# Last states of the first attention round gathered group by group, and the first table made ahead of the other setup work

## The chip, the cores and the metric

The kernel runs on one core of a Trainium2 chip. The metric is the device time of one execution in microseconds (us); of several runs the median is taken. The engines are PE (TensorE), DVE (VectorE), ACT (ScalarE), POOL (GpSimd) and SP (SyncE, which here only issues DMAs); ACT issues DMAs too, and POOL issues the indirect ones (gathers).

## The reference

A graph with 3125 nodes of 64 features and 103,125 edges sorted by destination goes through four blocks, each followed by a residual add and a layer norm: a normalised sum, two attention layers, a relational layer with 16 edge types and an edge convolution of three layers with a maximum. In short:

```python
edge_index = jnp.stack([src, dst])
x = _layernorm(x + _L0_gnn_ref(x, edge_index), axis=-1)      
x = _layernorm(x + _L1_gnn_ref(x, edge_index, edge_attr, ...))
x = _layernorm(x + _L2_gnn_ref(x, weight, norm, src, dst, rel_type), axis=-1)
x = _layernorm(x + _L3_gnn_ref(x, edge_index, W1, b1, W2, b2), axis=-1)

def _transformer_conv(...):          # one attention round
    ke = k[src] + e
    score = jnp.sum(q[dst] * ke, axis=-1) / jnp.sqrt(64)
    a = jnp.exp(score - jax.ops.segment_max(score, dst)[dst])
    alpha = a / jax.ops.segment_sum(a, dst)[dst]
    out = jax.ops.segment_sum(alpha[:, None] * (v[src] + e), dst)
    return out + x @ ws + bs
```

## The kernel before

Edges are padded to 808 tiles of 128 and taken in 202 chunks of 4 tiles (`TC`, `EC` = 512 edges). There are seven rounds, numbered from 0: sum, attention, attention, relation, and three maxima; in the maxima a step takes one chunk of either half, so that they have 101 steps. A round has two parts.

In its **chunk part** POOL gathers the source rows of a chunk from a table in HBM (`src_table`, four gathers of 128 rows each, L1086 or L1093), PE turns them so that features lie in partitions, DVE runs a scan along the edges (L1562) that starts anew where the destination changes, PE turns the scan's states back, ACT copies them to `hb`, and ACT's queue stores them to `states_sum` or `states_att` (L1236). A node's result is then the state of its last edge. In an attention round there is more: windows of `dst_table` are loaded by SP, one-hots on PE spread the queries to the edges, scores are formed and reduced per group of four chunks, and the weighted rows are scanned with a decay. Each engine has one instruction stream per round, written by `chunks` as a loop over a ring of 8 chunks (4 in the maxima), with stages that lag by up to 13 chunks; semaphores join the streams. In an attention round POOL may run 8 chunks ahead of the weighted rows (`q.weighted`).

In its **node part** the 25 blocks of 128 nodes are taken in 7 groups (`GROUPS`, six of four blocks and one of one). POOL gathers the last states of each block into `agg` by the indices `last_i` (L1114, 25 gathers). DVE, PE and ACT then form the next round's features in the order of `STEPS`, group after group, staggered, and SP stores them as the next `src_table` and `dst_table`. The next round's first gather waits for these.

POOL's wait ahead of these gathers differs by round:

```python
if g < G - 1 and q.r > 1:
    ends = [nc.values_load(group_ends[...]) for e, m in ((g, most), (G - 1 + g, least))]
    wait(pool, *[(q.st_stored[s], ends[0] if s < q.steps % U else ends[1]) for s in range(U)])
elif g == G - 1 or not g:
    wait(pool, *[(q.st_stored[s], each * ((q.steps - s + U - 1) // U)) for s in range(U)])
```

From round 2 on, group g waits only for the number of stored chunks that its own last edge needs (`group_ends`, made by DVE in the setup); in rounds 0 and 1, group 0 waits for all chunks of the round.

**Setup.** DVE counts per node how many tiles begin at or before it (L1453), POOL gathers the tile in which each node ends (L1077), and DVE counts within it (`count_within`, L1445 to L1448), three groups (`LATE`) behind. That gives `edges_le`, from it the degrees (with PE, and a square root on ACT) and `zn`, the features scaled by the inverse root degree, which SP stores as the first `src_table` (L943). Around it stand on DVE the tile-wise base `base` (which ACT needs for its first indices), the mask `joint`, the relation indices, `w1`, the flags `tile_same`, `last_i`, and later `tile_pens`. SP's queue is in order: loads, five stores of zero rows (`dst_table<-zrow`, L934), flags (L938, L940), the table (L943), the penalties `pens` (L945, L947), and then round 0, whose first loads are L962 and L965.

Of the kernel before, what the change touches and what calls it, by code (L numbers as in the profile page):

```python
# [26 lines left out]
P = 128  # L27
TC = 4
EC = TC * P
# [28 lines left out]
def gnn_kernel(nc, src, typ, wgt, dst_row, dst_prev, dst_tile, first, edge_t, x, W, out):  # L58
# [22 lines left out]
    with ctx:  # L81
# [15 lines left out]
        zrow = sb("zrow", [P, 3 * KA], bf16)  # L97
# [118 lines left out]
        zeros_stored = sem("zeros_stored")  # L216
        first_loaded = sem("first_loaded")
# [249 lines left out]
        PRE_EDGES = 2 + NB + 5 * G + 10  # L467
        PRE_DEG = PRE_EDGES + 4
        PRE_SCALED = PRE_DEG + 2

# [412 lines left out]
        def _(sp):  # L883
# [48 lines left out]
            for r in range(NR):  # L932
                if width[r]:
                    sp.dma_start(dsts[r][NP:NT, :], zrow[:, 0:3 * width[r]]).then_inc(zeros_stored, 16)  # L934

            sp.wait_ge(flags_made, 2)
# [5 lines left out]
            sp.wait_ge(dve_pre, PRE_SCALED)  # L942
            sp.dma_start(srcs[0].rearrange("(b p) f -> p b f", p=P), zn[:, :, :]).then_inc(rounds[0].src_stored[0], 16)  # L943
            sp.wait_ge(pens_made, 8)
            sp.dma_start(pens[0:whole * P, :].rearrange("(b p) f -> p b f", p=P), tile_pens[:, 0:whole, :])\  # L945
                .then_inc(pens_stored, 16)
            sp.dma_start(pens[whole * P:T, :], tile_pens[0:T - whole * P, whole, :]).then_inc(pens_stored, 16)  # L947

            for q in rounds:
# [88 lines left out]
                if k == SUM:  # L1038
                    chunks(sp, q.steps, (0, fetch_batch), (0, fetch_edges), (3, store_edges), (U + 2, store_onehots),
                           ring=2 * U)  # L1040
                elif k == REL:
# [10 lines left out]
        def _(pool):  # L1052
# [28 lines left out]
            for q in rounds:  # L1081
# [38 lines left out]
        def _(act):  # L1120
# [10 lines left out]
            nc.scalar.activation(deg[:, :], deg[:, :], ACT.Sqrt).then_inc(act_pre, 1)  # L1131

            for q in rounds:
# [117 lines left out]
                if k == ATT:  # L1251
                    chunks(act, q.steps, (B + 2, kept), (B + 2, weights), (B + LW, weigh), (B + LW, decays), (0, indices_att),
# [174 lines left out]
        def _(dve):  # L1427
# [23 lines left out]
            for g, (b0, nb) in enumerate(GROUPS):  # L1451
# [7 lines left out]
                if g >= LATE - 1:  # L1459
                    count_within(g - LATE + 1)  # L1460

            dve.wait_ge(pool_pre, PRE_POOL)
            dve.wait_ge(loaded, 16 * N_LOADS)
            pre(nc.vector.tensor_scalar(base[:, :], first_f[:, :], node_id[:, 0:1], None, ALU.add))
            pre(nc.vector.tensor_copy(before_f[:, :], before_half[:, :]))
            pre(nc.vector.tensor_tensor(before_f[:, :], before_f[:, :], first_f[:, TH:TH + 1], ALU.is_equal))
            pre(nc.vector.tensor_scalar(joint[:, :], node_id[:, :], first_f[:, TH:TH + 1], before_f[:, :],
                                        ALU.is_equal, ALU.mult))
            pre(nc.vector.tensor_scalar(joint[:, :], joint[:, :], BIG, -BIG, ALU.mult, ALU.add))
            pre(nc.vector.memset(edges_le[:, 0:1], 0.0))  # L1470
            pre(nc.vector.tensor_scalar(mask[:, :], src_i[:, :], float(R), None, ALU.mult))
            pre(nc.vector.tensor_tensor(mask[:, :], mask[:, :], rel_i[:, :], ALU.add))
            pre(nc.vector.tensor_copy(rel_i[:, :], mask[:, :]))
            pre(nc.vector.tensor_tensor(w1[:, :, 0:D], w1a[:, :, :], w1[:, :, D:2 * D], ALU.subtract))
# [7 lines left out]
            for g in range(G - LATE + 1, G):  # L1482
                count_within(g)
            assert made[0] == PRE_EDGES
            pre(nc.vector.tensor_scalar(last_f[:, :], edges_le[:, 1:NB + 1], -1.0, 0.0, ALU.add, ALU.max))
            pre(nc.vector.tensor_copy(last_i[:, :], last_f[:, :]))
            dve.wait_ge(pe_pre, 7)
            pre(nc.vector.tensor_tensor(deg[:, :], edges_le[:, 1:NB + 1], bank(2, 0)[:, 0:NB], ALU.subtract))
            pre(nc.vector.tensor_scalar(deg[:, :], deg[:, :], 1.0, None, ALU.max))
            assert made[0] == PRE_DEG  # L1490
            dve.wait_ge(act_pre, 7)
            pre(nc.vector.reciprocal(dinv[:, :], deg[:, :]))
            pre(nc.vector.tensor_tensor(zn[:, :, :], xn[:, :, :], dinv[:, :].unsqueeze(2).to_broadcast([P, NB, D]),
                                        ALU.mult))
            assert made[0] == PRE_SCALED

# [225 lines left out]
```

## Time and profile before

| | us |
|---|---|
| median of 3 runs | 9922.08 |
| the runs | 9895.71 to 9936.42 |
| profiled execution, span from first to last instruction | 9918.4 |

Of the profiled execution no other time is given than its span, so the two are taken as one and the same; it lies 3.7 us under the median of the runs. Its stages, by the first gather of each round: setup to 64 us, sum to 1345, first attention to 2986, second attention to 4722, relation to 5980, maxima to 7295, 8613 and the end.

A row of a timeline is one instruction, or several merged: its start, its duration, engine and line, result and operands, shapes, and in brackets how long the engine was idle before it and what ended that. "remote" and "another core or an unknown queue" mean that the trace names no releaser. SPq and ACTq rows are DMA issues, not the transfers.

### The profile page before, as it was taken

The numbers are of one execution on the slowest core, as the hardware profiler recorded it, in microseconds if no ns is written. First come the engines' busy times: TensorE is split into PE (matmuls) and PEld (weight loads), VectorE is DVE, ScalarE is ACT, GpSimd is POOL, SyncE is SP. The second block draws the span as 40 slices with busy tenths as digits, with TensorE's granted clock in tenths as the row PEclk, the third lists the DMA queues.
The fourth block names the chain that finished last, engine by engine and source line by source line (L and its number), as shares of the span: only waits on it lengthen the run. The fifth ranks groups of instructions, "written<-read, shape, count | busy, mean of one in ns | idle before, by whom it ended". The sixth has DMA issues, their size and how long they took to land.

```text
span 9918.4 us, 123616 instructions
## 1 busy us (share of the span) xinstructions
PE 3937.1 (40%) x24024; PEld 2674.1 (27%) x24024; DVE 2471.0 (25%) x4351; ACT 2035.1 (21%) x6406; POOL 5554.5 (56%) x5874
## 2 busy tenths in 40 slices
PE   2333334443343433336222224444444444444443
PEld 1222223333342333334111112222222222222222
DVE  4333333333332333332222221111111111111112
ACT  1111123333332333333101111111111111111111
POOL 6666644454434444442666665666656666556665
PEclk9999995555555555555555555666656666566666
DMA  4444434454444444443222223333333333333333
GB/s 121 126 126 126 125 91 108 109 110 107 108 92 97 109 106 107 107 107 99 54 50 50 51 48 82 91 90 90 89 79 90 90 90 90 80 89 90 91 91 80
DMA packets 2188624, 925.94 MB, mean 93 GB/s; under 512 B 1608302, under 2 KB 2071734, under 8 KB 2182134
## 3 DMA queue, kind: packets, MB, share of 16 engines
q1 hardware_dynamic: 1080022, 458.65, 19.0%
q10 hardware_dynamic: 921120, 272.38, 11.7%
q0 software_dynamic: 187392, 193.93, 9.6%
q8 instruction: 30, 0.49, 0.0%
q14 instruction: 60, 0.49, 0.0%
HBM read 657.48 MB, written 266.58 MB: 93 GB/s over the span
## 4 chain that ended last, share of the span: by engine, by line
issue 30%; PE 20%; another core or an unknown queue 9%; SPq 7%; DVE 2%; DVEq 1%; ACT 1%; DMA 0%; ACTq 0%; POOL 0%; POOLq 0%
PE ps L1323 7%; PE ps L1398 5%; PE ps L1319 3%; SPq L1002 3%; PE ps L1406 2%; PE ps L675 1%; PE ps L1309 1%; DVEq L374 1%; SPq L996 1%; SPq L1004 1%; SPq L998 1%; DVE edges_a L1580 1%; DVE st L1562 0%; SPq L370 0%
## 5 line engine op out<-in xcount | busy, mean ns | idle before, releaser
L1086 POOL DMA_INDIRECT edges_a<-src_table,idx x4040 | 3829.6, 948 | 2501.2 <-issue 1163.6
L1093 POOL DMA_INDIRECT edges_a<-src_table,idx x1616 | 1524.7, 944 | 1626.7 <-ACT weighted L1209 1063.1
L1323 PE MATMUL ps<-sel,win_sb 128*64 128x128 fp8e4 x7272 | 749.7, 262 | 1704.9 <-issue 1703.6
L1562 DVE TENSOR_TENSOR_SCAN st<-pen,st,ps 128x512 f32<-128x512 f32 x300 | 384.0, 1280 | 3279.9 <-remote 2939.6
L1406 PE MATMUL ps<-ident,st 64*128 64x64 f32 (+2 forms) x4444 | 849.1, 339 | 655.0 <-DVE st L1562 333.8
L1406 PEld LDWEIGHTS ps<-ident,st 64*128 64x128 f32 (+2 forms) x4444 | 705.6, 207 | 1063.1 <-issue 1039.8
L1323 PEld LDWEIGHTS ps<-sel,win_sb 128*64 128x64 bf16 x7272 | 396.2, 126 | 2056.6 <-issue 2009.9
L1562 DVE TENSOR_TENSOR_SCAN st<-edges_a,st,ps 64x512 f32<-64x512 fp8e4 x402 | 510.5, 1270 | 1665.6 <-remote 1292.0
L1309 PE MATMUL ps<-ident,edges_a 128*64 128x128 f32 x1616 | 421.4, 416 | 985.2 <-DVE edges_a L1580 643.5
L1335 PE MATMUL ps<-win_sb,sel 128*128 128x97 bf16 x4848 | 473.8, 271 | 849.1 <-issue 771.5
L1163 ACT ACTIVATE hb<-ps 128x256 f32<-128x256 f32 (+1 forms) x808 | 348.4, 431 | 2000.1 <-remote 1082.1
L1390 PE MATMUL ps<-ident,weighted 128*97 128x128 f32 x1616 | 452.8, 433 | 615.9 <-issue 279.9
L1595 DVE TENSOR_TENSOR prod<-ps,edges_a 128x388 f32<-128x388 f32 x404 | 225.4, 558 | 1795.3 <-remote 1459.7
L1335 PEld LDWEIGHTS ps<-win_sb,sel 128*128 128x128 fp8e4 x4848 | 396.1, 135 | 909.9 <-issue 826.0
L1319 PE MATMUL ps<-ident,edges_a 128*128 128x128 f32 x1212 | 439.2, 362 | 425.3 <-issue 354.7
L1227 ACT ACTIVATE edges_a<-ps,b 128x512 f32<-128x512 f32 x303 | 208.2, 687 | 1658.0 <-remote 1498.9
L1390 PEld LDWEIGHTS ps<-ident,weighted 128*97 128x97 f32 x1616 | 337.5, 274 | 659.9 <-issue 640.2
L1562 DVE TENSOR_TENSOR_SCAN st<-decay,st,ps 97x512 f32<-97x512 f32 x402 | 511.5, 1272 | 10.4 <-PE ps L1406 10.4
L1309 PEld LDWEIGHTS ps<-ident,edges_a 128*64 128x64 f32 x1616 | 216.4, 158 | 1063.7 <-issue 996.2
L1161 ACT ACTIVATE hb<-ps 128x512 f32<-128x512 f32 x303 | 180.9, 597 | 1555.4 <-issue 1386.1
L1398 PE MATMUL ps<-edges_a,w 128*128 128x512 f32 x606 | 481.9, 887 | 9.7 <-issue 8.0
L1209 ACT ACTIVATE weighted<-edges_a,weight 128x97 f32<-128x97 f32 x1616 | 471.9, 364 | 33.3 <-ACT hb L1163 23.9
(203 smaller groups left out, 3440.4 us busy)
## 6 DMA issues: line engine op xcount, KB each, us to landing
states_sum<-hb ACTq DMA_DIRECT2D x1010, 128.0 KB
win_sb<-dst_table SPq DMA_DIRECT2D x1616, 72.8 KB
edges_a<-src_table,idx POOLq DMA_INDIRECT x5656
states_att<-hb ACTq DMA_DIRECT2D x404, 194.0 KB
win_sb<-dst_table ACTq DMA_DIRECT2D x1212, 48.0 KB
win_sb<-dst_table SPq DMA_DIRECT2D x1212, 48.0 KB
dst_b<-in_dst_row SPq DMA_DIRECT2D x50, 1024.0 KB
sel<-onehots SPq DMA_DIRECT2D x303, 128.0 KB
```

What stands on the lines that cost most here:

```text
L1086: pool.indirect_dma_start(rows[:, s, j * D:(j + 1) * D], None, srcs[q.r], bass.IndirectOffsetOnAxis(ap=idx[:, s, j:j + 1], axis=0))\
L1093: pool.indirect_dma_start(xe_a[:, s, j * KA:j * KA + D], None, srcs[q.r], bass.IndirectOffsetOnAxis(ap=idx_a[:, s, j:j + 1], axis=0))\
L1163: nc.scalar.activation(hb[:, v, 0:TC * kw], bank(BACK, s)[:, 0:TC * kw], ACT.Copy)\
L1209: last = nc.scalar.activation(weighted[:, s % V, j * KA:(j + 1) * KA], xe_a[:, s, j * KA:(j + 1) * KA], ACT.Copy, scale=weight[:, gs_, o + ...
L1309: last = nc.tensor.matmul(bank(TURNED, s)[0:D, j * P:(j + 1) * P], rows[:, s, j * D:(j + 1) * D], ident[:, :], is_transpose=True, start=Tr ...
L1319: nc.tensor.matmul(bank(TURNED, s)[:, at_j], rows[:, s, j * P:(j + 1) * P], ident[:, :], is_transpose=True, start=True, stop=False)
L1323: last = nc.tensor.matmul(bank(TURNED, s)[h * D:h * D + D, at_j], win_pair(s, j, h)[:, i * D:(i + 1) * D], sel[:, s, h * EC + j * P:h * EC ...
L1335: last = nc.tensor.matmul(bank(TURNED, s)[:, j * KA:(j + 1) * KA], sel[:, v, j * P:(j + 1) * P], win_att(v, j)[:, i * KA:(i + 1) * KA], st ...
L1390: last = nc.tensor.matmul(bank(QUERY, s)[0:KA, j * P:(j + 1) * P], weighted[:, s % V, j * KA:(j + 1) * KA], ident[:, :], is_transpose=True ...
L1398: nc.tensor.matmul(bank(QUERY, s), w2[:, q.r - 4, :], xe[:, s, :], start=True, stop=True).then_inc(q.lifted.sem, 1)
L1406: last = nc.tensor.matmul(bank(BACK, s)[:, j * w:(j + 1) * w], st[0:w, s % V, j * P:(j + 1) * P], ident[0:w, 0:w], is_transpose=True, star ...
L1562: nc.vector.tensor_tensor_scan(st[0:w, s % V, :], d0, d1, init, op0, op1).then_inc(q.st_ready.sem, 1)
```

## The change

Three things are changed. (1) Round 1 waits group by group too: `q.r > 1` becomes `q.r > 0`. The gathers name the whole of `states_att`, whose end isn't written when the first ones go in round 1, so SP writes zeros to its last 24 chunks in the setup, and ACT waits for that ahead of the chunks of either attention round. (2) The setup on DVE is put in another order: the last two groups are counted first, then degrees, `dinv` and `zn`, then `base`, the flags, and all the rest. SP stores the table ahead of the flags, and ACT waits for `base` (`PRE_BASE`) ahead of round 0. (3) SP stores the penalties `pens` behind the chunks of round 0 and not ahead of them; round 1 is the first to read them.

```diff
-        zrow = sb("zrow", [P, 3 * KA], bf16)
+        zrow = sb("zrow", [P, 3 * KA + 1], bf16)
@@ SP, setup, behind the zero rows
+            tail = EP - LATE_CHUNKS * EC                 # LATE_CHUNKS = 24
+            sp.dma_start(states[1][tail:EP, :].rearrange("(p n) f -> p n f", p=P),
+                         zrow[:, :].bitcast(f32)[:, 0:KA].unsqueeze(1).to_broadcast([P, LATE_CHUNKS * TC, KA]))\
+                .then_inc(tail_cleared, 16)
+
+            sp.wait_ge(dve_pre, PRE_SCALED)
+            sp.dma_start(srcs[0]..., zn[:, :, :]).then_inc(rounds[0].src_stored[0], 16)
             sp.wait_ge(flags_made, 2)
             ...
-            sp.wait_ge(dve_pre, PRE_SCALED)
-            sp.dma_start(srcs[0]..., zn[:, :, :]).then_inc(rounds[0].src_stored[0], 16)
-            sp.wait_ge(pens_made, 8)
-            sp.dma_start(pens[0:whole * P, :]...)
-            sp.dma_start(pens[whole * P:T, :]...)
@@ SP, round 0
                     chunks(sp, q.steps, (0, fetch_batch), (0, fetch_edges), (3, store_edges), (U + 2, store_onehots),
                            ring=2 * U)
+                    sp.wait_ge(pens_made, 8)
+                    sp.dma_start(pens[0:whole * P, :]...)
+                    sp.dma_start(pens[whole * P:T, :]...)
@@ POOL, last states
-                    if g < G - 1 and q.r > 1:
+                    if g < G - 1 and q.r > 0:
@@ ACT
             nc.scalar.activation(deg[:, :], deg[:, :], ACT.Sqrt).then_inc(act_pre, 1)
+            act.wait_ge(dve_pre, PRE_BASE)
...
                 if k == ATT:
+                    act.wait_ge(tail_cleared, 16)
@@ DVE, setup, behind the loop over groups
+            pre(nc.vector.memset(edges_le[:, 0:1], 0.0))
+            for g in range(G - LATE + 1, G):
+                count_within(g)
+            dve.wait_ge(pe_pre, 7)
+            pre(...deg - shifted...), pre(...max(deg, 1)...)
             dve.wait_ge(pool_pre, PRE_POOL)
             dve.wait_ge(loaded, 16 * N_LOADS)
+            dve.wait_ge(act_pre, 7)
+            pre(nc.vector.reciprocal(dinv[:, :], deg[:, :]))
+            pre(nc.vector.tensor_tensor(zn[:, :, :], xn[:, :, :], dinv..., ALU.mult))
             pre(nc.vector.tensor_scalar(base[:, :], first_f[:, :], node_id[:, 0:1], None, ALU.add))
             dve.wait_ge(tiles_loaded, 64)
             ...tile_same (flags)...
+            ...before_f, joint, mask, rel_i, w1 (eight operations, moved from ahead of the flags)...
             pre(nc.vector.tensor_scalar(last_f[:, :], edges_le[:, 1:NB + 1], -1.0, 0.0, ALU.add, ALU.max))
             pre(nc.vector.tensor_copy(last_i[:, :], last_f[:, :]))
```

## Rows read from the trace of the kernel before

**Rows 1.** The page's first line: the span.

```profile
span 9918.4 us, 123616 instructions
```

**Rows 2.** Busy us of PE, PEld, DVE, ACT, POOL; clock, DMA share, GB/s: first attention round.

```profile
1345.00:2986.00 1641.00, 665.81 (x4597) 575.43 (x4597) 582.14 (x1067) 535.67 (x1906) 785.80 (x833) 0.57 0.48 104
```

**Rows 3.** POOL's timeline, end of the first attention round: start, us, instruction, idle before.

```profile
2913.80 0.94 POOL L1114 DMA_INDIRECT agg<-states_att,last_i  x1 [34.90 <-DMA states_att<-hb]
...
2943.76 0.94 POOL L1114 DMA_INDIRECT agg<-states_att,last_i  x1 [0.30 <-issue]
2986.13 0.94 POOL L1093 DMA_INDIRECT edges_a<-src_table,idx  x1 [41.43 <-ACT idx L1174]
```

**Rows 4.** DVE's timeline there: last scan, first normalised group.

```profile
2905.74 1.28 DVE L1562 TENSOR_TENSOR_SCAN st<-decay,st,ps 97x512 f32<-97x512 f32 x1 [0.77 <-PE ps L1406]
2920.09 0.18 DVE L830 RECIPROCAL ga<-agg 128x4 f32<-128x4 f32 x1 [13.07 <-DMA agg<-states_att,last_i]
```

**Rows 5.** Chain of work in the node stage there (start, us, what).

```profile
2933.67 14.84 another core or an unknown queue
```

**Rows 6.** POOL's timeline, end of the second attention round.

```profile
4535.27 0.94 POOL L1093 DMA_INDIRECT edges_a<-src_table,idx  x1 [0.30 <-issue]
...
4555.24 0.94 POOL L1114 DMA_INDIRECT agg<-states_att,last_i  x1 [0.30 <-issue]
...
4594.20 0.94 POOL L1114 DMA_INDIRECT agg<-states_att,last_i  x1 [29.23 <-DMA states_att<-hb]
```

**Rows 7.** DVE's timeline there.

```profile
4561.02 0.56 DVE L1595 TENSOR_TENSOR prod<-ps,edges_a 128x388 f32<-128x388 f32 x1 [27.94 <-remote]
...
4588.81 1.28 DVE L1562 TENSOR_TENSOR_SCAN st<-decay,st,ps 97x512 f32<-97x512 f32 x1 [0.77 <-PE ps L1406]
4590.01 0.15 DVE L830 RECIPROCAL ga<-agg 128x4 f32<-128x4 f32 x1
```

**Rows 8.** DVE's timeline, last scans of the sum and the relation round.

```profile
1282.16 1.26 DVE L1562 TENSOR_TENSOR_SCAN st<-edges_a,st,ps 64x512 f32<-64x512 fp8e4 x1
...
5926.93 1.27 DVE L1562 TENSOR_TENSOR_SCAN st<-edges_a,st,ps 64x512 f32<-64x512 fp8e4 x1 [1.23 <-issue]
```

**Rows 9.** POOL's timeline, first states of the sum, last rows of the relation round.

```profile
1287.60 0.94 POOL L1114 DMA_INDIRECT agg<-states_sum,last_i  x1 [14.29 <-DMA states_sum<-hb]
...
5901.60 0.94 POOL L1086 DMA_INDIRECT edges_a<-src_table,idx  x1 [0.30 <-issue]
```

**Rows 10.** DVE's timeline in the setup and at the first chunk.

```profile
46.25 0.89 DVE L1464 TENSOR_SCALAR base<-first_f,node_id 128x808 f32<-128x808 f32 x1
...
52.09 0.68 DVE L1445 TENSOR_TENSOR agg<-agg,node_id 128x512 f32<-128x512 int32 x1
...
54.37 0.16 DVE L1448 SCALAR_TENSOR_TENSOR edges_le<-tiles_le,within 128x1 f32<-128x1 f32 x1
...
56.85 1.82 DVE L1493 TENSOR_TENSOR zn<-xn,dinv 128x1600 f32<-128x1600 f32 x1
...
76.58 1.02 DVE L1569 TENSOR_SCALAR sel<-dst_b,nodes 128x128 fp8e4<-128x128 int32 x4 [5.91 <-DMA edges_a<-flags]
```

**Rows 11.** POOL's timeline in the setup.

```profile
47.04 0.94 POOL L1077 DMA_INDIRECT agg<-in_dst_tile,tile_i  x1 [0.30 <-issue]
64.13 1.56 POOL L1086 DMA_INDIRECT edges_a<-src_table,idx  x1 [16.14 <-DMA src_table<-zn]
```

**Rows 12.** Time to landing of destination-row gathers, 30 to 60 us.

```profile
DMA to landing us min/median/max: 2.9/2.9/2.9
```

**Rows 13.** SP's queue in the setup (a merged row gives its first start).

```profile
32.63 3.50 SPq L934 DMA_DIRECT2D dst_table<-zrow  x5
...
58.70 0.38 SPq L943 DMA_DIRECT2D src_table<-zn  x1
...
66.74 0.76 SPq L962 DMA_DIRECT2D dst_b<-in_dst_row  x1
```

**Rows 14.** DMA rate in 40 slices of 2900 to 2915 us.

```profile
GB/s 9 252 254 15 0 0 147 262 140 3 0 14 262 244 9 0 0 153 240 308 253 116 2 21 253 261 260 217 53 6 8 11 0 0 0 0 0 0 0 0
```

More of the change, by code:

```diff
@@ L216, in gnn_kernel @@
         zeros_stored = sem("zeros_stored")
+        tail_cleared = sem("tail_cleared")
         first_loaded = sem("first_loaded")
@@ L466, in gnn_kernel @@
         LATE = 3
-        PRE_EDGES = 2 + NB + 5 * G + 10
-        PRE_DEG = PRE_EDGES + 4
+        LATE_CHUNKS = 24
+        PRE_EDGES = 2 + NB + 5 * G + 1
+        PRE_DEG = PRE_EDGES + 2
         PRE_SCALED = PRE_DEG + 2
+        PRE_BASE = PRE_SCALED + 1
         def part(i, u, nb, w):
@@ L934, in _ @@
                     sp.dma_start(dsts[r][NP:NT, :], zrow[:, 0:3 * width[r]]).then_inc(zeros_stored, 16)
+            tail = EP - LATE_CHUNKS * EC
[3 more added lines that the diff above has]
+            sp.wait_ge(dve_pre, PRE_SCALED)
+            sp.dma_start(srcs[0].rearrange("(b p) f -> p b f", p=P), zn[:, :, :]).then_inc(rounds[0].src_stored[0], 16)
             sp.wait_ge(flags_made, 2)
@@ L1040, in _ @@
                            ring=2 * U)
+                    sp.wait_ge(pens_made, 8)
+                    sp.dma_start(pens[0:whole * P, :].rearrange("(b p) f -> p b f", p=P), tile_pens[:, 0:whole, :])\
+                        .then_inc(pens_stored, 16)
+                    sp.dma_start(pens[whole * P:T, :], tile_pens[0:T - whole * P, whole, :]).then_inc(pens_stored, 16)
                 elif k == REL:
@@ L1460, in _ @@
                     count_within(g - LATE + 1)
+            pre(nc.vector.memset(edges_le[:, 0:1], 0.0))
+            for g in range(G - LATE + 1, G):
+                count_within(g)
+            assert made[0] == PRE_EDGES
+            dve.wait_ge(pe_pre, 7)
+            pre(nc.vector.tensor_tensor(deg[:, :], edges_le[:, 1:NB + 1], bank(2, 0)[:, 0:NB], ALU.subtract))
+            pre(nc.vector.tensor_scalar(deg[:, :], deg[:, :], 1.0, None, ALU.max))
+            assert made[0] == PRE_DEG
             dve.wait_ge(pool_pre, PRE_POOL)
             dve.wait_ge(loaded, 16 * N_LOADS)
-            pre(nc.vector.tensor_scalar(base[:, :], first_f[:, :], node_id[:, 0:1], None, ALU.add))
[L1465 to L1474, printed above, removed]
+            dve.wait_ge(act_pre, 7)
+            pre(nc.vector.reciprocal(dinv[:, :], deg[:, :]))
+            pre(nc.vector.tensor_tensor(zn[:, :, :], xn[:, :, :], dinv[:, :].unsqueeze(2).to_broadcast([P, NB, D]),
+                                        ALU.mult))
+            assert made[0] == PRE_SCALED
+            pre(nc.vector.tensor_scalar(base[:, :], first_f[:, :], node_id[:, 0:1], None, ALU.add))
+            assert made[0] == PRE_BASE
             dve.wait_ge(tiles_loaded, 64)
@@ L1481, in _ @@
                 .then_inc(flags_made, 1)
-            for g in range(G - LATE + 1, G):
-                count_within(g)
-            assert made[0] == PRE_EDGES
+            pre(nc.vector.tensor_copy(before_f[:, :], before_half[:, :]))
+            pre(nc.vector.tensor_tensor(before_f[:, :], before_f[:, :], first_f[:, TH:TH + 1], ALU.is_equal))
+            pre(nc.vector.tensor_scalar(joint[:, :], node_id[:, :], first_f[:, TH:TH + 1], before_f[:, :],
+                                        ALU.is_equal, ALU.mult))
+            pre(nc.vector.tensor_scalar(joint[:, :], joint[:, :], BIG, -BIG, ALU.mult, ALU.add))
+            pre(nc.vector.tensor_scalar(mask[:, :], src_i[:, :], float(R), None, ALU.mult))
+            pre(nc.vector.tensor_tensor(mask[:, :], mask[:, :], rel_i[:, :], ALU.add))
+            pre(nc.vector.tensor_copy(rel_i[:, :], mask[:, :]))
+            pre(nc.vector.tensor_tensor(w1[:, :, 0:D], w1a[:, :, :], w1[:, :, D:2 * D], ALU.subtract))
             pre(nc.vector.tensor_scalar(last_f[:, :], edges_le[:, 1:NB + 1], -1.0, 0.0, ALU.add, ALU.max))
             pre(nc.vector.tensor_copy(last_i[:, :], last_f[:, :]))
[L1487 to L1495, printed above, removed]
             done = [0]
```

4 lines of the change are left out of this document (removed).

## The prediction

> **What bounds the kernel now.** I read the page's first line, then the busy times of the first attention round, then the timelines of GpSimd (POOL) and VectorE (DVE) where the two attention rounds end, the chain of work through the first of these ends, and last the setup. The span is 9918.4 us [rows 1]; the three runs have a median of 9922.1, so I work in microseconds of the profile and add 3.7 at the end. In the first attention round, 1641 us long, no engine is full: POOL is busy 785.8 us, PE 665.8, DVE 582.1, the DMA engines 0.48 of the time [rows 2]. A chunk is a loop of waits between them, and the change leaves its inside alone. What it touches are three seams: the setup (64 us), the end of the sum round and the end of the first attention round. So the question is how many of the some 80 us at that last end are saved, and the answer is bounded by rows.
>
> **The end of the first attention round, before.** POOL has issued its last row gather 34.90 us before 2913.80, at 2878.90; then it waits for the last chunk's states [rows 3]. The chunk pipeline drains until DVE's last scan ends at 2905.74 + 1.28 = 2907.02 [rows 4], so 28.1 us after POOL stopped. The first normalised group stands at 2920.09, with 13.07 us of idle before it [rows 4]. The 25 gathers of last states run from 2913.80 to 2944.70 [rows 3], 1.25 us apart. The node stage beside them then hangs for 14.84 us from 2933.67 [rows 5], to 2948.51, with no engine of this kernel named as releaser; POOL's last gather was issued 3.8 us before. The next round's first gather comes at 2986.13 [rows 3].
>
> **What the moved gathers save.** Of the 25, 20 (groups 0 to 4) need chunks up to 165 of 202 and are ready when POOL gets to them; group 5 ends in chunk 198 and waits nearly for the end. With 20 early, the first group need not wait: at most 13.07 us off. The hang of 14.84 us fell while the gathers were issued; with 5 gathers left at that point I expect it gone. The rest of the node stage (2986.13 − 2920.09 − 14.84 = 51.2 us) stays. Together −27.9 us; if the hang has another cause, −13.1.
>
> **What they cost.** The second attention round already does it this way, so it is the row to read. There the last row gather ends at 4536.21 and gathers of states follow at once, without a pause until 4556.2 [rows 6]. In the same stretch DVE stands still for 27.94 us before 4561.02, and the last scan ends at 4588.81 + 1.28 = 4590.09 [rows 7]: 53.9 us after POOL's last row gather, where the first attention round took 28.1. The node stage then starts at once, at 4590.01 [rows 7], as the saving above supposes, and the last 5 gathers follow at 4594.20 [rows 6], under it. So the same move costs 53.9 − 28.1 = 25.8 us of pipeline, which drains at a crawl while POOL issues. A second pair says the same more mildly: in the sum round, with gathers held back, 10.1 us pass from POOL's last row gather (1287.60 − 14.29 = 1273.31) to the end of the last scan (1283.42); in the relation round, with early gathers, 25.7 us (5902.54 to 5928.20) [rows 8, 9], 15.6 more, the two rounds being otherwise not quite alike. Bounds of this cost are 0 (the delay in the second round was chance) and 25.8; I take 25.8, since kind of round, tile shapes and the run of 8 row gathers ahead are the same. Net of the seam: −27.9 + 25.8 = −2.1 us. The register loads that each early group adds to POOL's queue are in the second round too, so its 25.8 us include them.
>
> **Setup.** Before, DVE goes from 46.25 through base, the joint mask and the relation indices, counts the last two groups between 52.09 and 54.53, waits for PE and ACT, and has zn at 56.85 + 1.82 = 58.67 [rows 10]. Now counting comes first. It could start at 46.35, but it needs POOL's gathers: the last is issued at 47.04 [rows 11] and lands 2.9 us later [rows 12], at 49.9; the four of the group before land at 48.7. From there 54.53 − 52.09 = 2.4 us of counting give 51.1, and the unchanged chain of 4.1 us (54.53 to 58.67) gives zn at 55.3, 3.4 us earlier. The two operations on last rows and the rest fall behind, inside a DVE that waited 5.91 us for its first chunk at 76.58 [rows 10]. The table takes 5.4 us from its store at 58.70 [rows 13] to POOL's first gather at 64.13 [rows 11]; that gather would come at 60.7. ACT's new wait for base ends at 56.2 and is covered by it. SP used to reach the first chunk's loads at 66.74 [rows 13], behind flags, table and pens; now the pens (811 KB) are gone from there, and it waits for the flags alone, which are issued behind the table and land near 61. So both feeds of chunk 0 come 3.4 to 5.4 us earlier; I take 3.4.
>
> **The cleared tail** is new work: 24 × 512 rows of 388 bytes, 4.77 MB, in SP's queue behind the zero rows (32.63 + 3.50 = 36.1 [rows 13]). The same packets, written by the attention rounds' stores, move at 253 to 262 GB/s where the engines are full [rows 14], so 18 to 19 us: it ends at 54.8 to 55.1, just when zn is ready at 55.3. It shares the engines with the last gathers of destination rows; if those land 1 us later, so does zn. I take 1 us off the gain for it: setup −2.4. Its bounds: 0, and the whole 3.4 and more (rival 3). The Trainium skill, "DMA: Bandwidth & Descriptors", under "Queues, rings and completion order", says that each DMA engine takes the descriptors of one queue in ring order and alternates between queues. By that the table's store, on the same queue, starts only when the clear is through, while POOL's gathers slip in between; at the measured rate both readings give the same time, and no row of before shows it.
>
> **The pens store** at the end of the sum round puts 811 KB into SP's queue when the last chunk's loads are out, and nothing waits for it before the attention round, some 60 us later (1283.42 to 1345): 0, or 5.4 us, what the table's 800 KB take above, if it were in the way of a node store. ACT's wait for the clear is met over 1200 us before ACT comes to it: 0.
>
> **Sum:** −2.1 − 2.4 = −4.5 us on the profile, 9913.9; by the median 9917.6.
>
> **Rivals.** (1) *Free tail*, 0.15: the crawl in the second round was chance and the first drains in 28 us again: −27.9 − 2.4 = −30.3, 9892. Against it stand the two pairs of rows above. (2) *The hang stays*, 0.14: the 14.84 us are not due to the gathers, and the tail pays 25.8: −13.1 + 25.8 − 2.4 = +10.3, 9932. For it speaks that the releaser is unnamed; against it, that the second round's crawl and this hang both end some 4 to 5 us after POOL's run of gathers. It turns slower as soon as the tail costs over 15.5 us. (3) *The clear is late*, 0.12: it goes at half the rate, 37 us, and holds the table's store until 73.5 instead of 55.3; gathers start at 79, +15 us: −2.1 + 15 = +13, 9935. It turns slower once the clear needs over 24 us. The Trainium skill, same page, "Specifications", says that below 512 bytes the engines read, modify and write; but the 388-byte rows measured above carry that already. (4) *Nothing happens*, 0.09: group ends round up so that even early groups wait for the last chunk; then only the setup counts, 9920. The second round's gathers without a pause speak against it. My forecast, the exchange, has 0.50. None of these alone passes 0.5% (50 us), about what a measurement of this kernel can tell from no change, as its runs lie 41 us apart.
>
> **Range.** From the free tail (9892) and the late clear (9935), widened by half the spread of the runs (20 us) on both sides: 9872 to 9955. The likeliest case by itself holds 9898 to 9938. For over 0.5% either way a rival has to meet the runs' spread on its side: faster 0.07, slower 0.06, within 0.87.
>
> **What would show it.** Right: POOL's gathers of states in the first attention round start at once behind its last row gather, 20 in a row; DVE's last scan ends 50 to 57 us after POOL's last row gather, not 28; the first normalised group directly behind the last scan; no hang over 5 us in that node stage, and 50 to 53 us from its start to the next round's first gather; first gather of all at 60 to 63 us; the clear through before 58. Wrong: a drain of 28 to 35 us (rival 1), the hang still there (rival 2), first gather behind 66 (rival 3). The forecast as a whole fails if loops elsewhere get a new chunk time: 1% of the first attention round's 1641 us is 16 us.

## The result and the profile after

The changed kernel has a median of 9924.66 us (9892.61 to 9952.02, 20 runs) against 9894.7 us of the kernel before on the same chip (9884.8 to 9936.42, 20 runs): ratio 1.0023, 95% interval [1.0015, 1.0032]. It is a little slower, by 15 to 32 us by that interval, where the forecast was 4.5 us faster. The profiled execution spans 16.2 us more, 9934.6 against 9918.4.

```profile
span 9934.6 us, 123670 instructions
```

The loss stands in the setup. SP's queue there (start, us of issue), beside [rows 13]:

```profile
37.19 0.01 SPq L939 DMA_DIRECT2D states_att<-zrow  x1
64.22 9.20 SPq L944 DMA_DIRECT2D src_table<-zn  x1
73.45 7.73 SPq L947 DMA_DIRECT2D flags<-tile_same  x1
81.23 0.48 SPq L949 DMA_DIRECT2D flags<-tile_same  x1
83.66 0.36 SPq L964 DMA_DIRECT2D dst_b<-in_dst_row  x1
```

and DVE's and POOL's timelines, beside [rows 10] and [rows 11]:

```profile
51.46 0.69 DVE L1453 TENSOR_TENSOR agg<-agg,node_id 128x512 f32<-128x512 int32 x1 [4.73 <-DMA agg<-in_dst_tile,tile_i]
...
57.56 0.69 DVE L1453 TENSOR_TENSOR agg<-agg,node_id 128x512 f32<-128x512 int32 x1 [4.37 <-DMA agg<-in_dst_tile,tile_i]
...
62.36 1.83 DVE L1482 TENSOR_TENSOR zn<-xn,dinv 128x1600 f32<-128x1600 f32 x1
```

```profile
83.34 0.94 POOL L1092 DMA_INDIRECT edges_a<-src_table,idx  x1 [33.21 <-DMA src_table<-zn]
```

The view of DMAs from 34 to 54 us gives the rate in slices of 0.5 us, and for each kind of transfer its size and the median time from issue to landing:

```profile
GB/s 218 158 127 30 0 47 203 232 254 193 121 116 116 146 83 141 81 102 127 113 113 151 104 154 141 143 152 144 98 124 145 170 118 120 192 81 172 148 154 157
...
states_att<-zrow SPq DMA_DIRECT2D x1, 4656.0 KB, 44.0
...
agg<-in_dst_tile,tile_i POOLq DMA_INDIRECT x9, 9.5
```

The clear is issued at 37.19 and lands 44.0 us later, at 81.2. It goes at 193 to 254 GB/s for four slices (37 to 39 us) and then at 81 to 192, 131 in the mean, with all that goes beside it. From 64 to 72 us, when no gather runs beside it, it makes 104 to 112 GB/s; over its whole life the 4.77 MB make 108 GB/s. The gathers of destination rows beside it land after 9.5 us where they took 2.9 [rows 12], and DVE waits 4.73 and 4.37 us for two groups of them, so that zn is ready at 62.36 + 1.83 = 64.19 and not at 58.67. From the store of the table to POOL's first gather 19.1 us pass (64.22 to 83.34) and not 5.4; issuing the store alone holds SP for 9.20 us, where it took 0.38 [rows 13]. Together 5.5 + 13.7 = 19.2 us, which is the first gather's delay, 83.34 against 64.13.

The end of the first attention round went as forecast. POOL and PE there, beside [rows 3], and DVE, beside [rows 4]:

```profile
2892.09 0.94 POOL L1099 DMA_INDIRECT edges_a<-src_table,idx  x1 [0.30 <-issue]
2893.34 0.94 POOL L1120 DMA_INDIRECT agg<-states_att,last_i  x1 [0.30 <-issue]
...
2919.46 0.94 POOL L1120 DMA_INDIRECT agg<-states_att,last_i  x1 [0.31 <-issue]
2954.83 0.94 POOL L1120 DMA_INDIRECT agg<-states_att,last_i  x1 [34.42 <-DMA states_att<-hb]
...
2998.69 0.94 POOL L1099 DMA_INDIRECT edges_a<-src_table,idx  x1 [37.93 <-ACT idx L1181]
```

```profile
2893.10 0.78 PE L1343 MATMUL ps<-win_sb,sel 128*128 128x97 bf16 x7
2895.42 0.24 PE L1343 MATMUL ps<-win_sb,sel 128*128 128x97 bf16 x1 [1.55 <-issue]
2896.82 0.24 PE L1343 MATMUL ps<-win_sb,sel 128*128 128x97 bf16 x1 [1.16 <-issue]
2898.92 0.24 PE L1343 MATMUL ps<-win_sb,sel 128*128 128x97 bf16 x1 [1.86 <-issue]
2901.02 0.24 PE L1343 MATMUL ps<-win_sb,sel 128*128 128x97 bf16 x1 [1.86 <-issue]
2902.42 0.24 PE L1343 MATMUL ps<-win_sb,sel 128*128 128x97 bf16 x1 [1.16 <-issue]
2923.97 0.38 PE L1353 MATMUL ps<-ident,score 128*16 128x128 f32 x1 [21.32 <-DVE score L1608]
```

```profile
2922.76 0.56 DVE L1604 TENSOR_TENSOR prod<-ps,edges_a 128x388 f32<-128x388 f32 x1 [31.39 <-remote]
...
2947.86 1.28 DVE L1571 TENSOR_TENSOR_SCAN st<-decay,st,ps 97x512 f32<-97x512 f32 x1 [0.77 <-PE ps L1414]
2949.05 0.15 DVE L833 RECIPROCAL ga<-agg 128x4 f32<-128x4 f32 x1
```

Twenty gathers of states follow the last row gather at once, with one pause of 2.7 us. In that time PE, which needs 0.78 us for seven multiplications at 2893.10, issues the remaining five of that chunk one by one, 1.40 or 2.10 us apart, without a wait that the profile shows; DVE stands still for 31.39 us. The last of the five is through at 2902.66, and what holds DVE for another 20 us the profile does not name. In the code this product waits for PE's queries, for the chunk's gathered rows and for its edge rows; the trace gives no landing time for either transfer here. DVE goes on 2.4 us after POOL's twentieth gather ended. The last scan ends at 2949.14, 56.1 us after the last row gather; the node part starts at once and takes 49.6 us to the next round's first gather, with no hang in it: the longest pieces of its chain of work are PE's own, 5.0 us each. Before, 28.1 + 79.1 = 107.2 us; now 56.1 + 49.6 = 105.7.

### The profile page after: what moved, and what is told of

Same layout as the page of the kernel before. It is cut to its first block, busy times and chain, and to the rows that moved or that the text cites. A ratio compares the mean times of both kernels' runs of the same rounds, so it can differ in the third digit from the quotient of the medians.

```text
span 9934.6 us, 123670 instructions
## 1 busy us (share of the span) xinstructions
PE 3940.0 (40%) x24024; PEld 2674.2 (27%) x24024; DVE 2470.1 (25%) x4351; ACT 2036.4 (20%) x6406; POOL 5552.5 (56%) x5874
## 4 chain that ended last, share of the span: by engine, by line
issue 40%; PE 24%; another core or an unknown queue 15%; SPq 13%; DVE 4%; DVEq 2%; DMA 1%; ACT 1%; ACTq 1%; POOL 0%; POOLq 0%
PE ps L1331 7%; SPq L1004 6%; PE ps L1406 5%; PE ps L1414 3%; PE ps L1327 3%; PE ps L1317 2%; SPq L998 2%; SPq L1006 1%; SPq L1000 1%; DVEq L375 1%; DVE st L1571 1%; PE ps L678 1%; SPq L375 1%; DVE edges_a L1589 1%
```

## The experiments

They ran in four groups, each on one chip and with its own runs of the kernel before there. Ratios are to those runs: 10089.12 us for the first group, 9915.85 for the second, 7656.42 for the third, 9920.15 for the fourth; clear_one_row and clear_two_rows were timed once, beside 7649.64 on a fifth chip. That a chip runs the same kernel in 7650 us and another in 9920 is taken up below. In this table a seam is the drain (end of POOL's last row gather to end of the last scan) + the node part (from there to the next round's first gather), both from the timelines, in us and exact to about 0.1; "clear" is its time from issue to landing, "first gather" the start of POOL's first row gather. Every seam is that of one profiled execution.

| kernel | ratio, interval | clear | first gather | first attention seam | second |
|---|---|---|---|---|---|
| before (first profile) | 1 | none | 64.1 | 28.1 + 79.1 | 53.9 + 132.1 |
| changed | 1.0023 [1.0015, 1.0032] | 44.0 | 83.3 | 56.1 + 49.6 | 54.0 + 134.6 |
| setup_only | 0.9993 [0.9984, 1.0003] | none | 60.7 | 28.1 + 79.5 | 50.5 + 134.0 |
| clear_only | 1.0019 [1.0010, 1.0028] | 45.4 | 85.4 | 28.3 + 79.2 | 54.3 + 123.1 |
| clear_by_rows | 1.0009 [0.9999, 1.0018] | 34.8 | 72.9 | 54.3 + 49.5 | 50.9 + 136.8 |
| clear_long | 0.9997 [0.9988, 1.0006] | 13.5 | 63.7 | 50.0 + 49.5 | 50.8 + 132.9 |
| paced | 0.9962 [0.9947, 0.9977] | not shown | 61.4 | 28.2 + 59.7 | 28.3 + 144.0 |
| two_early | 0.9993 [0.9983, 1.0003] | 14.0 | 64.0 | 39.4 + 63.3 | 39.2 + 140.9 |
| held_both | 1.0005 [0.9996, 1.0014] | none | 60.9 | 28.2 + 79.8 | 28.2 + 158.9 |
| clear_half | 1.0003 [0.9994, 1.0012] | 23.5 | 69.2 | 54.7 + 49.6 | 54.0 + 127.0 |
| before_twin (9910.78) | | none | 63.8 | 27.4 + 79.0 | 56.0 + 130.4 |
| after_twin | 1.0015 [1.0006, 1.0024] | 43.9 | 82.2 | 54.2 + 49.5 | 56.1 + 129.1 |
| pace_second_twin | 0.9980 [0.9969, 0.9991] | none | 65.8 | 28.2 + 79.1 | 28.3 + 139.5 |
| pace_earlier_twin | 0.9963 [0.9949, 0.9978] | 14.1 | 63.2 | 33.8 + 56.3 | 33.8 + 137.0 |
| *7650-us chips:* pace_second | 1.0000 [0.9991, 1.0009] | none | 63.8 | 25.3 + 63.1 | 22.2 + 128.2 |
| pace_earlier | 0.9979 [0.9970, 0.9988] | 14.6 | 60.7 | 23.4 + 49.5 | 22.6 + 134.5 |
| clear_one_row (7672.35) | | 51.8 | 87.5 | 23.8 + 50.1 | 23.0 + 136.8 |
| clear_two_rows (7646.44) | | 30.2 | 67.4 | 22.9 + 49.8 | 23.7 + 132.0 |

### Which part loses

**setup_only** is the changed kernel without the clear and with round 1 waiting as before:

```diff
-            sp.dma_start(states[1][tail:EP, :]..., zrow...).then_inc(tail_cleared, 16)
-                    act.wait_ge(tail_cleared, 16)
-                    if g < G - 1 and q.r > 0:
+                    if g < G - 1 and q.r > 1:
```

> The changed kernel without the clear and without the group-by-group gathers of the first attention round: what is left is the new order of the setup and the pens store behind the sum round. My theory (the clear alone makes the setup late): POOL's first gather comes at 60 to 62 us in place of 64.1, span 3 to 6 us under before. Rival (the new order itself is late, since DVE counts the last two groups before anything else and waits for POOL's gathers): first gather at 66 or later, and the time not under before.

**clear_only** is the kernel before with nothing but the clear and ACT's wait:

```diff
+            sp.dma_start(states[1][tail:EP, :]..., zrow...).then_inc(tail_cleared, 16)   # SP, behind the zero rows
+                    act.wait_ge(tail_cleared, 16)
```

> The kernel before plus the clear of 24 chunks in SP's queue behind the zero rows, and ACT's wait for it. My theory: the clear takes some 40 us by itself as in the changed kernel (44 us from issue to landing), and table and flags, which are behind it in the queue, land behind it: first gather at 80 to 84 us, +16 to +20 us on the span, the whole loss of the changed kernel. Rival (the loss came from the new order meeting the clear: there the gathers of destination rows, 9.5 us to landing, were on the path): with the old order DVE has other work to do meanwhile, so that the first gather comes at 70 us or before, and the time is at most 8 us over before.

The new setup order alone has zn ready at 55.2 us and the first gather at 60.71, where the forecast had 55.3 and 60.7:

```profile
53.36 1.82 DVE L1477 TENSOR_TENSOR zn<-xn,dinv 128x1600 f32<-128x1600 f32 x1
```

```profile
60.71 0.94 POOL L1088 DMA_INDIRECT edges_a<-src_table,idx  x1 [12.54 <-DMA src_table<-zn]
```

The clear alone costs 0.19% and puts the first gather off to 85.39. So the order is worth its 3.4 us in the trace (its ratio, 0.9993, cannot be told from 1) and the whole loss is the clear's; that the old order would cover it did not hold.

### Why the clear is slow

**clear_by_rows** deals the rows to partitions in turn, so that neighbouring packets come from different partitions:

```diff
-            ...states[1][tail:EP, :].rearrange("(p n) f -> p n f", p=P)
+            ...states[1][tail:EP, :].rearrange("(n p) f -> p n f", p=P)
```

> The changed kernel, with the clear's rows dealt out the other way: neighbouring rows of the table come from neighbouring partitions, as in the stores of states, and not 96 in a row from one partition. Same number of packets, same source. Theory A (the rate of 108 GB/s comes from where the packets are written: one engine writes neighbouring unaligned rows): the clear goes at 200 GB/s or more, 24 us or less to landing, first gather at 66 us or before, time 15 us under the changed kernel. Theory B (it is the rate that such small packets have when they go on for longer than a few us, or the repeated read of one row): again 40 us or more, same time as the changed kernel.

34.8 us lie between the two theories: the order of the rows has a part in it, 9.2 us, not the main one. The gathers beside it still land after 9.1 us.

**clear_long** writes the same bytes in runs of 16 rows (6208 bytes) from a zeroed part of `hb`; ACT waits for it ahead of round 0:

```diff
+            pool.memset(hb[:, :, :].rearrange("p u f -> p (u f)")[:, 0:16 * KA], 0.0).then_inc(hb_zero, 1)
-            ...rearrange("(p n) f -> p n f", p=P), zrow[...]...to_broadcast([P, LATE_CHUNKS * TC, KA])
+            ...rearrange("(p k n) f -> p k (n f)", p=P, k=6), hb[...][:, 0:16 * KA]...to_broadcast([P, 6, 16 * KA])
```

> The changed kernel, with the clear written from a zeroed stretch of hb (16 rows, 6208 bytes in each partition), so that its packets are 16 times as long, and ACT waiting for it ahead of the sum round. My theory (the number of short packets is what the clear costs): it lands 12 to 18 us after its issue, the gathers of destination rows land within 4 us, first gather at 61 to 64 us, and the kernel is 15 to 20 us faster than the changed one and 3 to 8 us faster than before (setup 3, seam 2). Rival (it is the bytes, 4.77 MB, or anything else in the path): no more than 5 us better than the changed kernel.

```profile
GB/s 134 121 118 91 25 0 131 323 422 422 397 372 435 372 372 310 384 467 422 392 459 380 409 422 459 459 397 410 410 397 348 335 344 131 33 82 16 0 0 0
...
states_att<-hb SPq DMA_DIRECT2D x1, 4656.0 KB, 13.5
...
agg<-in_dst_tile,tile_i POOLq DMA_INDIRECT x9, 2.9
```

The clear now goes at 310 to 467 GB/s in most slices and lands in 13.5 us, the gathers beside it after 2.9 us again, and the first gather comes at 63.73. The changed kernel's loss is gone (0.9997). **clear_half** left the packets short and cleared 12 chunks in place of 24 (`LATE_CHUNKS = 12`):

> The changed kernel with 12 chunks cleared and not 24. My theory (the clear costs its 12288 short packets at some 115 GB/s, and the table is late by what is left of it when zn is ready): clear lands some 22 us after its issue, first gather at 62 to 66 us, 15 us less than the changed kernel. Rival (a fixed cost of having it in the queue): first gather behind 75 us.

Half the bytes took 23.5 us, 101 GB/s; with that the first gather is at 69.2 and the ratio 1.0003. The clear is through at 59.1 there, ahead of the table's store at 63.7, so what is left of the delay comes from the gathers of destination rows, which land after 10.2 us and hold zn up.

clear_long had changed the source with the packets. Two kernels tell these apart: both are clear_long with shorter runs, **clear_one_row** with one row (388 bytes), **clear_two_rows** with two (776):

```diff
-            ...rearrange("(p k n) f -> p k (n f)", p=P, k=6), hb[...][:, 0:16 * KA]...to_broadcast([P, 6, 16 * KA])
+            ...rearrange("(p k) f -> p k f", p=P),            hb[...][:, 0:KA]...to_broadcast([P, LATE_CHUNKS * TC, KA])
+            ...rearrange("(p k n) f -> p k (n f)", p=P, k=48), hb[...][:, 0:2 * KA]...to_broadcast([P, 48, 2 * KA])
```

> The long clear with its source and start kept (zeroed hb, behind POOL's memset) and its packets as short as in the change: 388 bytes, 96 to a partition. If the short packets are what makes the clear slow (theory A), it lands 40 to 46 us after its issue and the destination-row gathers beside it take 9 to 10 us. If it was the source zrow (theory B), it lands as in the long clear, 13 to 16 us after its issue.

> The same with packets of two rows, 776 bytes, 48 to a partition. Theory A1, there is a step at 512 bytes: 13 to 16 us to landing, as with 6208 bytes. Theory A2, each packet has a price of its own whatever its length: half as many packets, so half the time of one_row, 20 to 23 us, and the gathers beside it at 5 to 9 us.

```profile
states_att<-hb SPq DMA_DIRECT2D x1, 4656.0 KB, 51.8
agg<-in_dst_tile,tile_i POOLq DMA_INDIRECT x9, 11.2
```

```profile
states_att<-hb SPq DMA_DIRECT2D x1, 4656.0 KB, 30.2
```

51.8 us with the new source and 388 bytes, more even than the 40 to 46 expected: the source is out of it. 30.2 us with 776 bytes is no step down to 14, and not quite the half; neither theory's figure was met. The two times differ by 21.6 us for 6144 packets fewer, 3.5 ns for each packet of the transfer, over 8.6 us that do not depend on their number; by that line the 768 packets of clear_long would take 11.3 us (13.5 to 14.6 measured). The line goes through two single runs on one chip; on the chips of the changed kernel and of clear_half the same packets took 44.0 and 23.5 us, 3.3 ns for each. The Trainium skill, "DMA: Bandwidth & Descriptors", under "Specifications", gives 512 bytes as the least size for full rate. The runs agree that 388 bytes are far from it, but 776 are too: 158 GB/s against 353 with 6208.

What the packets of the clear cost is not the price of every short packet. The table's store, in the kernel before, writes 3200 packets of 256 bytes, and the view of 56 to 66 us (slices of 0.25 us) has it almost alone:

```profile
GB/s 0 0 0 0 0 0 0 0 0 0 0 0 0 0 46 242 217 218 219 217 218 217 217 218 218 217 218 218 217 158 1 0 0 0 0 0 0 0 0 0
DMA packets 3216, 0.82 MB, mean 82 GB/s; under 512 B 3216, under 2 KB 3216, under 8 KB 3216
```

That is 218 GB/s or 1.2 ns for each packet, held for 3.5 us, a third of the clear's price. Its packets are shorter, but there are a quarter as many; each comes from a row of its own, where the clear reads one row of each partition 96 times; and its rows begin at multiples of 256 bytes in their table, which rows of 388 bytes do not. Which of these differences counts, no run separates. Shown is that fewer and longer packets from the same tile, with the same number of bytes written, take the loss away.

### What the early gathers cost

**held_both** has the new setup order, no clear, and holds the gathers back in both attention rounds (`q.r > 2`):

> The changed kernel without the clear and with both attention rounds held back as the first one was before (group by group only from the relation round on). My theory (an even exchange: 22 to 26 us of slower drain for 28 us of waiting and hang): in the second attention round the last scan comes 28 us after POOL's last row gather and not 50 to 54, the node stage begins 13 us later and hangs, and the time is within 0.1% of the kernel with only the new setup. Rival (the long drain of the second round has another cause, as that round's other tables): it stays over 45 us.

The second seam is 187.0 us against 186.0 with early gathers in the kernel before: 25.7 us of drain are bought with 26.8 us of node part. So the exchange is about even. It is not known closer than that, since the second seams of the kernels with twenty early gathers lie between 177.4 and 188.6 us, and clear_half, on held_both's own chip, has 181.0.

**two_early**, on clear_long, has only the first two groups (8 gathers) early; **paced**, on clear_long too, spreads the first five groups over the drain:

```diff
+                    if q.kind == ATT and g == 2:                                        # two_early
+                        wait(pool, *[(q.st_stored[s], each * ((q.steps - s + U - 1) // U)) for s in range(U)])
```

```diff
+                    if q.kind == ATT and g < G - 2:                                     # paced
+                        last_c = 191 + 2 * g
+                        wait(pool, (q.st_stored[last_c % U], each * (last_c // U + 1)))
```

> The kernel with the clear in long packets, where in both attention rounds only the first two groups (8 gathers) are gathered early and the third waits for all chunks. Theory A (the length of the run counts): the run is 16 gathers and not 28, the drain takes 35 to 42 us; the first group needs no wait, but 17 gathers now lie beside the node stage, where the hang of some 15 us comes back in part. Seam 95 to 105 us. Theory B (every gather of states beside the drain costs its 1.25 us): drain 38 us as well, but no hang in the node stage: seam 90 us. Node stage of 60 to 68 us speaks for A, 50 for B.

> The kernel with the clear in long packets, and in both attention rounds group g of the first five waits in addition until chunk 191 + 2g is stored, so that the 20 early gathers come four at a time between the last chunks and not in a run. Theory A (the run of gathers without a pause is what slows the drain of the pipeline): last scan 28 to 36 us after POOL's last row gather in both attention rounds, in place of 50 to 56, node stage still 50 us, each attention seam 15 to 22 us shorter than 100 to 106 us, and the time 0.3 to 0.4% under the kernel before. Theory B (any gather of states beside the drain costs what it saves): seams of 100 us or more, same time as with long packets alone.

Eight gathers in a row lengthen the drain by 11.2 us (39.4 against 28.2), twenty by 22 to 28; that is 1.1 to 1.4 us for each, and POOL issues one in 1.25 us. So the drain is put off by about the time that POOL spends on issuing. With two_early the node part is 63.3 us and not 49.5, as its theory A had it: with the other gathers beside the node part, pieces of 4.1 and 8.2 us without a named releaser stand in its chain of work. Paced, the drain is 28.2 us again, though ten gathers lie inside it; the other fifteen follow behind the last scan:

```profile
2868.39 0.95 POOL L1102 DMA_INDIRECT edges_a<-src_table,idx  x1 [0.31 <-issue]
2878.03 0.95 POOL L1126 DMA_INDIRECT agg<-states_att,last_i  x1 [8.69 <-DMA states_att<-hb]
...
2886.18 0.95 POOL L1126 DMA_INDIRECT agg<-states_att,last_i  x1 [3.46 <-DMA states_att<-hb]
...
2894.51 0.95 POOL L1126 DMA_INDIRECT agg<-states_att,last_i  x1 [3.63 <-DMA states_att<-hb]
...
2957.18 0.94 POOL L1102 DMA_INDIRECT edges_a<-src_table,idx  x1 [40.61 <-ACT idx L1188]
```

```profile
2897.45 0.15 DVE L834 RECIPROCAL ga<-agg 128x4 f32<-128x4 f32 x1
```

The first attention seam falls from 107.2 to 87.9 us and the second from 186.0 to 172.3, 33.0 us together, which is most of what the ratio gives (38 us). The paced kernel beats both: 0.9962 [0.9947, 0.9977]. Pacing alone, on the kernel before and in the second attention round only (`if q.r == 2 and g < G - 2`), and pacing that begins two chunks earlier (`189 + 2 * g`), were run on two chips each:

> The kernel before, its setup and first attention round untouched; only in the second attention round do the gathers of group g, for the first five groups, also wait until chunk 191 + 2g is stored. Pacing is what helps (theory A): drain from the last row gather to the last scan 28 us instead of 53.9, node part 140 to 146 us instead of 132.1, so 14 to 18 us off, ratio 0.998 to 0.999. The gain of the paced kernel came from its setup and its long clear together with chance (theory B): 0.9995 to 1.0005.

> The paced kernel with both attention rounds starting two chunks earlier: group g waits for chunk 189 + 2g. If the 10 us that the paced node part took over the unpaced one (59.7 against 49.6 us) are due to gathers that end late (theory A), they shrink to 0 to 5 us, with the drain still 28 to 32 us: ratio to before 0.995 to 0.9965, 3 to 10 us under the paced kernel. If gathers that come nearer to the last row gathers make a long run with these again (theory B), the drain grows to 35 us or more and nothing is won: 0.9965 to 0.998.

> The kernel before once more, for its trace on this chip; the last call's chip ran it in 7656 us, where POOL's gathers never paused and PE's 12 multiplications of one chunk followed at once. Theory A, the crawl belongs to the chip: where the median is near 7650 the trace shows gathers 1.25 us apart all through a round and a second drain of 22 to 25 us; where it is near 9900 it shows a second drain of 50 to 57 us. Theory B, the crawl belongs to the kernel's long runs of gathers on any chip: drain of 45 us or more in both cases.

> The changed kernel once more. On a chip with the crawl: ratio to before 1.001 to 1.003, as measured. On a chip without it: theory A, the early gathers cost nothing there, so the seam of the first attention round is 20 to 28 us shorter, and the clear costs its 15 to 20 us in the setup as before: ratio 0.999 to 1.000. Theory B, the seam stays as it was and the clear costs as much: 1.002 to 1.003.

> The kernel before with paced gathers in the second attention round alone. On a chip with the crawl: theory A, drain 28 us instead of 53.9 and node part 140 to 146 instead of 132.1, ratio 0.998 to 0.999; theory B, pacing did nothing by itself, 0.9995 to 1.0005. On a chip without the crawl both expect 0.9995 to 1.001.

> Long clear, setup order and pacing from chunk 189 on in both attention rounds. On a chip with the crawl: theory A, 0.995 to 0.9965 (paced kernel 0.9962), with a drain of 28 to 32 us and a node part of 50 to 57 us in the first attention round; theory B, gathers that come nearer to the row gathers crawl again, drain over 35 us, 0.9965 to 0.998. On a chip without the crawl: 0.998 again.

In the third group neither theory was tested as meant, since that chip runs the kernel before in 7656 us. Rows of pace_second in the middle of an attention round there, POOL and PE together:

```profile
2001.82 0.94 POOL L1093 DMA_INDIRECT edges_a<-src_table,idx  x1 [0.30 <-issue]
...
2002.69 1.19 PE L1338 MATMUL ps<-win_sb,sel 128*128 128x97 bf16 x12
...
2003.07 0.94 POOL L1093 DMA_INDIRECT edges_a<-src_table,idx  x1 [0.30 <-issue]
```

and POOL's group of row gathers in the second attention round (busy us, mean ns, idle before and what ended it), in the kernel before on the first chip and in pace_second on this one:

```profile
L1093 POOL DMA_INDIRECT edges_a<-src_table,idx x807 | 761.3, 943 | 828.9 <-ACT weighted L1209 526.6 <-issue 243.1 <-ACT idx L1174 59.2
```

```profile
L1093 POOL DMA_INDIRECT edges_a<-src_table,idx x805 | 760.4, 945 | 273.4 <-issue 223.2 <-ACT idx L1177 33.7 <-ACT weighted L1212 16.2
```

The gathers are as long on both (943 and 945 ns), but here POOL waits for weighted rows 16.2 us in the round and not 526.6, and PE issues all twelve multiplications of a chunk in 1.19 us while POOL issues gather after gather. The twelve by themselves tell little, since they come as fast on the first chip beside some short runs of gathers; the waits and the drains tell it. So the slow issue belongs to some chips and not to the kernel alone. Where it is absent, twenty early gathers in a row cost nothing: clear_two_rows has them unpaced, and its last scan ends 22.9 us after the last row gather, with the first normalised group at once:

```profile
2155.31 0.94 POOL L1102 DMA_INDIRECT edges_a<-src_table,idx  x1 [0.30 <-issue]
2156.55 1.00 POOL L1123 DMA_INDIRECT agg<-states_att,last_i  x1 [0.30 <-DMA states_att<-hb]
...
2180.34 1.05 POOL L1123 DMA_INDIRECT agg<-states_att,last_i  x1 [0.30 <-issue]
```

```profile
2177.82 1.28 DVE L1574 TENSOR_TENSOR_SCAN st<-decay,st,ps 97x512 f32<-97x512 f32 x1 [0.77 <-PE ps L1417]
2179.01 0.15 DVE L834 RECIPROCAL ga<-agg 128x4 f32<-128x4 f32 x1
```

Its first attention seam is 72.7 us, against 88.4 in pace_second, which holds the gathers back in that round: 15.7 us saved, and pacing has nothing to add there (pace_earlier 72.9). The fourth group's chip has the slow issue, and there pacing the second round alone gives 0.9980 [0.9969, 0.9991], its seam 167.7 us against 186.4 in before_twin. Pacing from two chunks earlier gives 90.1 us in the first seam where 87.9 stood: a drain of 33.8 in place of 28.2, a node part 3.4 us shorter, and no difference in the ratio (0.9963 and 0.9962). after_twin repeats the result, 1.0015, with the clear at 43.9 us and the first gather at 82.2. Not tried were a kernel with early gathers and no clear at all, and one that clears in short packets from another queue or behind the table's store.

## Why the prediction was wrong

- **Where it failed: the cleared tail.** The term took 18 to 19 us for 4.77 MB, at 253 to 262 GB/s from [rows 14], with the end at 54.8 to 55.1 and 1 us off the gain of the setup. Measured: 44.0 us, the end at 81.2, and −2.4 us became +19.2. [rows 14] shows bursts of 0.8 to 2.3 us, one or two chunks' stores of 194 KB each. The clear also began at 193 to 254 GB/s and held it for 2 us only. A rate of bursts was taken for one that lasts 19 us; twenty-four such stores back to back, which the clear amounts to, had no row. With the 21.6 us that this term is off, the sum of −4.5 becomes +17.1, against +16.2 in the spans.
- **The closeness of the number is luck.** The forecast of 9917.6 us lies 7.1 us under the measured 9924.66. It stood on three runs of the kernel before with a median of 9922.08; twenty runs put it at 9894.7, and that 27 us stands in for the rise that was not foreseen.
- **The size of "1 us later"** for the destination-row gathers was part of the same error: they landed 6.6 us later (9.5 against 2.9), and zn 8.9 us behind the forecast's 55.3 (64.2).
- **Rival 3 is what happened**, at a chance of 0.12: half rate, 37 us, the table's store held, first gather at 79, +15 us. Measured 44.0, 83.3 and +19.2. Its turning point of 24 us fits clear_half, which needed 23.5 us and stands at 1.0003, but by another way: there the late gathers held zn up and the clear no longer held the store. By the Trainium skill, "DMA: Bandwidth & Descriptors", "Queues, rings and completion order", as the prediction weighed it under the cleared tail, the table's store starts behind the clear, and POOL's gathers slip between. The trace agrees: the store issued at 64.22 lands at 83.1, 1.9 us after the clear, while the gathers from another queue landed all along, only later.
- **The setup order** was right: 55.3 and 60.7 forecast, 55.2 and 60.7 in setup_only.
- **The seam** was right step by step. Last scan 50 to 57 us after the last row gather: 56.1. Node part 50 to 53 us: 49.6, since the first group came at once (the 13.07 us) and the hang of 14.84 was gone. −2.1 forecast for the seam, −1.6 measured. Why the drain slows was left open by the prediction and is open still. Rivals 1 and 2 (free tail, the hang stays) and 4 (nothing happens) did not come in the profiled kernel. Rival 1 is what a chip without the slow issue shows, where the drain stays at 22.9 us and the seam gives 15.7 us.
- **The pens store**, taken as 0: the sum's seam is 71.6 us after and 71.4 before.
- **What is not accounted for**: of the 19.2 us, 15.0 are left at the first attention round's first gather and 16.2 at the end, and the twins' spans lie 29.1 us apart with the first gathers 18.4 apart. Rounds that the change does not touch differ from profile to profile: the sum's seam by up to 6.6 us over eleven profiles.

Why the clear's short packets sustain so little is open, and so is what makes PE and DVE crawl beside POOL's gathers on some chips and not on others.

## What to carry to other kernels

A rate read from bursts of about 2 us is a bound, not a price, for a transfer ten times as long: ask how many packets it has and what shares the queues, and write a fill in runs as long as the tile allows. A filler store off the critical path is not free when the one store that everything waits for stands behind it in the same queue. Early gathers bring a gain only if the pipeline beside them goes on; spread them over the drain instead of issuing them in one run.

## What the runs showed of the hardware

- The clear's 388-byte packets went at 193 to 254 GB/s for about 2 us, then near 110; its 4.77 MB took 43.9 to 51.8 us in such packets (34.8 with the rows dealt in turn), 30.2 in 776-byte ones and 13.5 to 14.6 in 6208-byte ones. The table's store kept 218 GB/s with 256-byte packets for 3.5 us. Beside the packets of 388 and 776 bytes, gathers from another queue landed after 9.1 to 11.2 us in place of 2.9; beside the longest after 2.9 us in clear_long and paced and after 5.5 to 6.9 in two_early and the two runs of pace_earlier.
- A store issued behind the clear in the same queue held SP for 9.20 us in place of 0.38 and landed 1.9 us after it.
- On the chips that take 9900 us and more, in a long run of gathers 1.25 us apart, five of PE's multiplications came 1.40 or 2.10 us apart with no wait in the profile, and the drain grew by 1.1 to 1.4 us for each gather; on the two chips that take 7650 us twelve of them came in 1.19 us beside such a run, and the drain did not grow.
- Those two kinds of chips ran one and the same kernel in 7650 and in 9900 to 10,090 us: between the row gathers of one attention round POOL was idle for 273.4 us in the one and 828.9 in the other.
